# Layer 3's input transform partly as butterflies on VectorE, and y's columns moved forward

## The reference, cut to what matters

```python
x = input.reshape(-1, n)
x = fwht(x * SU_ug) / SCALE                     # n = 512
x_up   = x @ W_up.T   * (Wscale_ug[:INTER] * SCALE)
x_gate = x @ W_gate.T * (Wscale_ug[INTER:] * SCALE)
x = jax.nn.silu(x_gate) * x_up
x = fwht(x * SU_dp) / SCALE                     # n = 2048
x = x @ W_down.T * (Wscale_dp * SCALE)
```

## Time and profile before

| | us |
|---|---|
| median of 3 runs | 1746.19 |
| the runs | 1741.15 to 1750.22 |
| span of the profiled execution, first to last instruction | 1737.0 |
| TensorE busy in it | 1523.9 (88%) |
| VectorE busy | 1123.6 (65%) |
| ScalarE busy | 968.9 (56%) |
| GpSimd busy | 379.1 (22%) |

### The profile page before, as it was taken

One profiled execution on the slowest core, in us unless ns is written; L12 is line 12 of the kernel. 1 busy time (PEld: TensorE's weight loads), 2 busy tenths in 40 slices (PEclk: granted clock), 3 DMA queues, 4 the chain that ended last, 5 costly groups with the idle time before them and its releaser, 6 DMA issues.

```text
span 1737.0 us, 19550 instructions
## 1 busy us (share of the span) xinstructions
PE 1523.9 (88%) x6486; PEld 977.9 (56%) x6486; DVE 1123.6 (65%) x1830; ACT 968.9 (56%) x1270; POOL 379.1 (22%) x306
## 2 busy tenths in 40 slices
PE   5676587789995899997789999699999999999997
PEld 2222234344442456664644444378888888888886
DVE  7899488899996889995877777854322222222222
ACT  6765488889994689997347777643321221221211
POOL 0000011111110211110034545551231321321311
PEclk9898789999998899999789999889999999999999
DMA  7765633312211787763935454570110100100001
GB/s 284 267 209 187 223 115 103 110 43 79 66 39 48 210 223 182 182 164 96 367 112 182 144 184 142 196 255 13 37 37 1 37 29 9 37 15 22 1 25 73
DMA packets 102997, 206.16 MB, mean 119 GB/s; under 512 B 11060, under 2 KB 27956, under 8 KB 99188
## 3 DMA queue, kind: packets, MB, share of 16 engines
q1 hardware_dynamic: 90308, 173.72, 29.1%
q0 software_dynamic: 12592, 31.20, 8.0%
HBM read 140.13 MB, written 52.17 MB: 111 GB/s over the span
## 4 chain that ended last, share of the span: by engine, by line
PE 48%; DVE 2%; DMA 1%; ACT 1%; issue 0%; POOL 0%; SPq 0%; DVEq 0%; POOLq 0%; ACTq 0%
PE ffn_po L2502 10%; PE ffn_pg L2483 10%; PE ffn_pu L2483 10%; PE moe_psum L1890 8%; PE moe_psum L1911 4%; PE ffn_po L1584 2%; PE ffn_po L1571 2%; PE moe_psum L1829 1%; PE moe_psum L1878 1%; DVE x L2572 1%; PE moe_psum L1901 0%; DMA in_part<-expert_out,moe_source 0%; DVE x L1617 0%; DVE rt_hot_block L2183 0%; DMA rt_consts<-in_route 0%
## 5 line engine op out<-in xcount | busy, mean ns | idle before, releaser
L2405 ACT ACTIVATE up_front<-ffn_pg,ffn_gate_chunk 128x512 f32<-128x512 f32 x64 | 44.1, 689 | 320.7 <-PE ffn_pg L2483 271.7
L2562 DVE SCALAR_TENSOR_TENSOR up_front<-ffn_pu,ffn_up_scale,up_front 128x512 f32<-128x512 f32 x64 | 48.0, 751 | 231.6 <-PE ffn_pu L2483 231.5
L2572 DVE SCALAR_TENSOR_TENSOR x<-ffn_po,ffn_out_scale,x 128x512 f32<-128x512 f32 x128 | 87.2, 744 | 148.1 <-PE ffn_po L2502 148.1
L2456 POOL TENSOR_TENSOR ffn_hl<-up_front,ffn_hh 128x512 fp32r<-128x512 f32 x64 | 82.8, 1295 | 396.4 <-ACT ffn_hh L2412 396.4
L942 POOL TENSOR_TENSOR l_rr<-l_rr,constants 128x1 f32<-128x1 f32 x32 | 28.9, 903 | 487.3 <-DVE l_rr L969 487.3
L2502 PE MATMUL ffn_po<-ffn_hh,ffn_wh 128*128 128x512 f32 x256 | 101.3, 396 | 4.2 <-DVE x L2572 2.9
L2483 PE MATMUL ffn_pg<-zhi,ffn_wh 128*128 128x512 f32 x256 | 101.5, 397 | 0.5
L2483 PE MATMUL ffn_pu<-zhi,ffn_wh 128*128 128x512 f32 x256 | 100.9, 394 | 0.0
L2502 PE MATMUL ffn_po<-ffn_hh,ffn_wl 128*128 128x512 f32 x256 | 100.6, 393 | 0.0
L2483 PE MATMUL ffn_pg<-zhi,ffn_wl 128*128 128x512 f32 x256 | 100.4, 392 | 0.0
L2483 PE MATMUL ffn_pu<-zhi,ffn_wl 128*128 128x512 f32 x256 | 100.4, 392 | 0.0
(11 more groups left out here) (353 smaller groups left out, 4039.5 us busy)
## 6 DMA issues: line engine op xcount, KB each, us to landing
wkv_k<-in_fside SPq DMA_DIRECT2D x64, 256.0 KB, 4.4
ratio<-wkv_fn SPq DMA_DIRECT2D x64, 256.0 KB, 2.3
wkv_ek<-exp_k SPq DMA_DIRECT2D x48, 256.0 KB, 2.9
wkv_ekv<-exp_k_times_v SPq DMA_DIRECT2D x48, 256.0 KB, 3.5
expert_out<-moe_eo SPq DMA_DIRECT2D x39, 256.0 KB, 2.0
up_front<-in_gated SPq DMA_DIRECT2D x8, 1024.0 KB, 5.0
x<-in_x SPq DMA_DIRECT2D x4, 1024.0 KB, 7.6
down_first_a<-in_down_raw SPq DMA_DIRECT2D x16, 256.0 KB, 2.7
```

Source lines behind the costliest of these rows:

```text
L2405: eng.activation(hf[t], p_g[t][:, :], ACT.Silu, scale=scale).then_inc(*E(f"silu{t}").inc)
L2456: eng.tensor_tensor(hl[t][slot % 2][:, :], hf[t], hh[t][slot % 2][:, :].bitcast(F32), ALU.subtract).then_inc(*E(f"hl{t}").inc)
L2562: eng.scalar_tensor_tensor(hf[t], p_u[t][:, :], scale, hf[t], ALU.mult, ALU.mult).then_inc(*E(f"h{t}").inc)
L2572: last = eng.scalar_tensor_tensor(x[:, o, :], p_o[:, o, :], out_s[:, o:o + 1], x[:, o, :], ALU.mult, ALU.add)
```

## The change

The 4-point transform over the channel tiles moves from TensorE to VectorE, before the rounding. `inner` adds and subtracts tiles 0 and 1, and 2 and 3; `outer` combines the results. The sums are made in place in `g`, with the k=0 half of the diagonal matrices as spare room (these are now one allocation). ScalarE's rounding waits for `outer`, and the tiles come in the order 2, 0, 3, 1. TensorE's `fwht` keeps the 128-point part, 4 x 2 = 8 products. The matrix minus H and the instruction that made it are gone. On TensorE the columns of y of batch i+1 (`next_cols`) move from behind the "up" product of t=0 to ahead of it, for i = 0, 1 and 2.

```diff
+AS_MADE = (2, 0, 3, 1)
...
-        self.minus_H = sb("in3_minus_H", [P, P], F32R)
-        self.diag = [[sb(f"in3_diag{k}_{t}", [P, P]) for t in range(TPB)] for k in range(2)]
+        diag = sb("in3_diag", [P, 2, TPB, P])
+        self.diag = [[diag[:, k, t, :] for t in range(TPB)] for k in range(2)]
+        self.spare = diag[:, 0, :, :].rearrange("p t n -> p (t n)")
...
     def fwht(self, eng, i):
-        eng.wait_ge(*self.E("minus_H").at(0))
         eng.wait_ge(*self.E("x").at(CT * i + CT - 1))
-        for k in range(CT):
-            eng.wait_ge(*self.E("z_low").at(CT * i + k))
-            for j in range(CT):
-                h = self.minus_H if (k & j).bit_count() % 2 else self.c["H128"]
-                for t, part in enumerate((self.high(i), self.low(i))):
-                    last = eng.matmul(self.banks[:, j, :], h[:, :], part[:, k, :],
-                                      start=(k + t == 0), stop=(k == CT - 1 and t == 1))
-                if k == CT - 1:
-                    last.then_inc(*self.E("fwht").inc)
+        for n, j in enumerate(AS_MADE):
+            eng.wait_ge(*self.E("z_low").at(CT * i + n))
+            for t, part in enumerate((self.high(i), self.low(i))):
+                last = eng.matmul(self.banks[:, j, :], self.c["H128"][:, :], part[:, j, :], start=t == 0, stop=t == 1)
+            last.then_inc(*self.E("fwht").inc)
...
     def z_high(self, eng, n):
-        eng.wait_ge(*self.E("z").at(n))
-        eng.activation(self.high(n // CT)[:, n % CT, :], self.g[n % CT][:, :], ACT.Copy).then_inc(*self.E("z_high").inc)
+        k = AS_MADE[n % CT]
+        eng.wait_ge(*self.E("outer").at(n))
+        eng.activation(self.high(n // CT)[:, k, :], self.transformed(k), ACT.Copy).then_inc(*self.E("z_high").inc)
...
     def gate_and_round(self, eng, i):
         n = CT * i
-        self.gate(eng, n)
         for k in range(CT):
-            if k + 1 < CT:
-                self.gate(eng, n + k + 1)
+            self.gate(eng, n + k)
+        for k in range(CT):
             self.z_high(eng, n + k)
...
+    def inner(self, eng, i, pair):
+        eng.wait_ge(*self.E("z").at(CT * i + 2 * pair + 1))
+        if pair:
+            eng.wait_ge(*self.E("inner").at(CT * i + 1))
+        even, odd = (self.g[2 * pair + k][:, :] for k in range(2))
+        apart = self.g[1] if pair else self.spare
+        eng.tensor_tensor(apart, even, odd, ALU.subtract).then_inc(*self.E("inner").inc)
+        eng.tensor_tensor(even, even, odd, ALU.add).then_inc(*self.E("inner").inc)
+
+    def transformed(self, j):
+        return self.g[(0, 1, 3, 2)[j]][:, :]
+
+    def outer(self, eng, i):
+        eng.wait_ge(*self.E("inner").at(CT * i + CT - 1))
+        g = [t[:, :] for t in self.g]
+        eng.tensor_tensor(g[3], g[0], g[2], ALU.subtract).then_inc(*self.E("outer").inc)
+        eng.tensor_tensor(g[0], g[0], g[2], ALU.add).then_inc(*self.E("outer").inc)
+        eng.wait_ge(*self.E("outer").at(CT * i + 1))
+        eng.tensor_tensor(g[2], self.spare, g[1], ALU.subtract).then_inc(*self.E("outer").inc)
+        eng.tensor_tensor(g[1], self.spare, g[1], ALU.add).then_inc(*self.E("outer").inc)
...
     def gated(self, eng, i):
...
         self.z(eng, n + 1)
-        self.z_low(eng, n)
         self.residual(eng, n + 3)
         self.z(eng, n + 2)
-        self.z_low(eng, n + 1)
+        self.inner(eng, i, 0)
         self.z(eng, n + 3)
-        self.z_low(eng, n + 2)
-        self.z_low(eng, n + 3)
+        self.inner(eng, i, 1)
+        self.outer(eng, i)
+        for k in range(CT):
+            self.z_low(eng, n + k)
...
             product(0, 0, "gate", 0)
+            next_cols(1)
             product(0, 0, "up", 0)
-            next_cols(1)
             product(0, 0, "gate", 1)
...
             product(1, 1, "gate", 0)
+            next_cols(2)
             product(1, 1, "up", 0)
-            next_cols(2)
...
             product(2, 2, "gate", 0)
+            next_cols(3)
             product(2, 2, "up", 0)
-            next_cols(3)
```

More of the change, by code:

```diff
@@ L1523, in __init__ @@
         self.e = {}
-        self.minus_H, self.su, self.diag = start.minus_H, start.su_ug, start.diag
+        self.su, self.diag, self.spare = start.su_ug, start.diag, start.spare
         own = [start.parts, [core.sb(scope, f"in3_part{t}", [P, CH], F32)[:, :] for t in range(TPB)]]
@@ L1561, in diagonals @@
                 weight = self.c["moe_weight"][:, i * TPB + t, k:k + 1]
-                last = eng.tensor_scalar(self.diag[k][t][:, :], self.c["ident"][:, :], weight, None, ALU.mult)
+                last = eng.tensor_scalar(self.diag[k][t], self.c["ident"][:, :], weight, None, ALU.mult)
         last.then_inc(*self.E("diag").inc)
@@ L1571, in cols_of_y @@
                     last = eng.matmul(self.banks[:, o, t * P:(t + 1) * P], self.parts[i % 2][k][t][:, o * P:(o + 1) * P],
-                                      self.diag[k][t][:, :], start=k == 0, stop=k == 1)
+                                      self.diag[k][t], start=k == 0, stop=k == 1)
                 if t == TPB - 1:
@@ L1591, in gate @@
         if n >= CT:
-            eng.wait_ge(*self.E("z_low").at(n - CT))
+            eng.wait_ge(*self.E("z_low").at(n // CT * CT - 1))
         eng.activation(self.g[n % CT][:, :], self.x(n), ACT.Sigmoid).then_inc(*self.E("gate").inc)
     def z_high(self, eng, n):
-        eng.wait_ge(*self.E("z").at(n))
-        eng.activation(self.high(n // CT)[:, n % CT, :], self.g[n % CT][:, :], ACT.Copy).then_inc(*self.E("z_high").inc)
+        k = AS_MADE[n % CT]
+        eng.wait_ge(*self.E("outer").at(n))
+        eng.activation(self.high(n // CT)[:, k, :], self.transformed(k), ACT.Copy).then_inc(*self.E("z_high").inc)
     def gate_and_round(self, eng, i):
         n = CT * i
-        self.gate(eng, n)
         for k in range(CT):
-            if k + 1 < CT:
-                self.gate(eng, n + k + 1)
+            self.gate(eng, n + k)
+        for k in range(CT):
             self.z_high(eng, n + k)
     def round_transformed(self, eng, i):
-        for j in range(CT):
-            eng.wait_ge(*self.E("fwht").at(CT * i + j))
+        for n, j in enumerate(AS_MADE):
+            eng.wait_ge(*self.E("fwht").at(CT * i + n))
             eng.activation(self.high(i)[:, j, :], self.banks[:, j, :], ACT.Copy).then_inc(*self.E("high").inc)
-    def constants(self, eng):
-        eng.tensor_scalar(self.minus_H[:, :], self.c["H128"][:, :].bitcast(F32), -1.0, None, ALU.mult).then_inc(*self.E("minus_H").inc)
     def residual(self, eng, n):
@@ L1625, in z @@
         eng.scalar_tensor_tensor(g, g, self.su[:, k:k + 1], ratio, ALU.mult, ALU.mult).then_inc(*self.E("z").inc)
+    def inner(self, eng, i, pair):
[16 more added lines that the diff above has]
+        eng.tensor_tensor(g[1], self.spare, g[1], ALU.add).then_inc(*self.E("outer").inc)
     def z_low(self, eng, n):
-        k, g = n % CT, self.g[n % CT][:, :]
+        k = AS_MADE[n % CT]
         eng.wait_ge(*self.E("z_high").at(n))
-        eng.tensor_tensor(self.low(n // CT)[:, k, :], g, self.high(n // CT)[:, k, :].bitcast(F32), ALU.subtract).then_inc(*self.E("z_low").inc)
+        eng.tensor_tensor(self.low(n // CT)[:, k, :], self.transformed(k), self.high(n // CT)[:, k, :].bitcast(F32), ALU.subtract).then_inc(*self.E("z_low").inc)
     def gated(self, eng, i):
@@ L1638, in gated @@
         self.z(eng, n + 1)
-        self.z_low(eng, n)
         self.residual(eng, n + 3)
         self.z(eng, n + 2)
-        self.z_low(eng, n + 1)
+        self.inner(eng, i, 0)
         self.z(eng, n + 3)
-        self.z_low(eng, n + 2)
-        self.z_low(eng, n + 3)
+        self.inner(eng, i, 1)
+        self.outer(eng, i)
+        for k in range(CT):
+            self.z_low(eng, n + k)
     def low_transformed(self, eng, i):
-        for j in range(CT):
-            eng.wait_ge(*self.E("high").at(CT * i + j))
+        for n, j in enumerate(AS_MADE):
+            eng.wait_ge(*self.E("high").at(CT * i + n))
             eng.tensor_tensor(self.low(i)[:, j, :], self.banks[:, j, :], self.high(i)[:, j, :].bitcast(F32), ALU.subtract).then_inc(*self.E("low").inc)
@@ L2478, in product @@
                 n = 0
-                for k in range(CT):
+                for m, k in enumerate(AS_MADE):
                     if i < BATCH:
-                        eng.wait_ge(*inp.E("low").at(CT * i + k))
+                        eng.wait_ge(*inp.E("low").at(CT * i + m))
                     for part, z in ((wh, inp.zhi), (wh, inp.zlo), (wl, inp.zhi)):
```

1 line of the change is left out of this document (removed).

## The result

| | before | changed |
|---|---|---|
| median | 1743.67 us (1739.81 to 1750.22, 4 runs) | 1756.53 us (1754.65 to 1759.58, 4 runs) |
| ratio | | 1.0078, 95% interval 1.005 to 1.0105 |
| span of the profiled execution | 1737.0 | 1752.4 |

The account below looks back on a forecast made before the run. TensorE, busy 88%, bounds the kernel, but the queue order on VectorE and ScalarE decides the change: queues +8.5, clock +2.8, GpSimd +0.5, total +11.8, on span 1737.0 gives 1748.8, plus 9.2 gives 1758.0 us; range 1746 to 1765.

Parts of the forecast that it names:

- the stretch: Layer 3's input from S0 to the first product of batch 3; queues alone were forecast to lengthen it by 8.5 us.
- Rival 1: TensorE's work decides and VectorE's chain hides behind its products: 16.8 us gained, 1729.4 us; chance 0.07.
- S0 to S1: From batch 0's first product to batch 1's: forecast 32.1 us against 25.95 before, +6.1.
- S0: Start of batch 0's first product in layer 3 (S1, S2, S3: batches 1, 2, 3); forecast unshifted, near 1149.6.
- R: Start of a batch's first residual on VectorE; in batch 1 forecast at S0+13.6, where it was S0+11.58.
- S1 to S2: From batch 1's first product to batch 2's: forecast 34.7 us against 32.72 before, +2.0.
- S2 to S3: From batch 2's first product to batch 3's: forecast 33.1 us against 32.71 before, +0.4.
- The clock: TensorE's products run at 1.2 GHz in place of 2.4 after new idle stretches: +2.8 us, bounds 0 and +3.6.
- GpSimd: Its low part of batch 0's hidden tile falls among batch 1's butterflies and lengthens them: +0.5 us, bounds 0 and +1.3.
- Rival 3: GpSimd's instructions catch the butterflies in every batch: 3 x 1.3 more in place of 0.5, 1761.4 us; chance 0.11.
- The base of the sum: Span 1737.0 us plus 9.2 for launch and noise up to the median of 1746.19, to which the shift was added.
- queues: Order of VectorE's and ScalarE's instructions delays the first residuals and the transform's rounding: +8.5 us, bounds +7 and +33.

Follow-up runs that it names:

- cols_alone: Kernel before with only y's columns moved ahead of the up product of t=0, 32 products a batch, no butterflies: 1.0084 times before.
- queue: Changed kernel with VectorE's and ScalarE's queues reordered so the next batch's input stands first: 1725.96 us, 0.9951 times before.
- queue_old_transform: Kernel before with columns moved and both queues reordered, next batch's input first, but 32 products and no butterflies: 1735.10 us, 0.9996 times before.
- cols_back: Changed kernel with y's columns put back behind the up product of t=0, butterflies kept: 1.0039 times before.
- the changed kernel again: Changed kernel measured once more without any edit, on another chip: 1747.18 us, 1.0072 times before.
- keep_busy_all: Changed kernel with unread products filling TensorE's new waits, including the one behind batch 1's transform: 1745.54 us, 1.0064 times before.
- gather_later: Changed kernel with GpSimd making the low part of batch 0's hidden tile of t=0 ahead of the last gathers: 1753.43 us, single execution.
- front_only: Changed kernel with only the next batch's residuals and gates moved ahead of hidden of t=0 and its rounding: 0.9997 times before.
- back_only: Changed kernel with only the transform's rounding and low parts moved ahead of the diagonals, hidden of t=1 and its rounding: 1.005 times before.
- keep_busy: Changed kernel with unread products in TensorE's new idle stretches, but none behind batch 1's transform: 1.0082 times before.

## Why the prediction was right, point by point

The direction, the mechanism and the size held: 1758.0 was forecast and 1756.53 measured. As a shift, +11.8 was forecast, and 12.9 measured between the medians and 13.2 in the stretch. That the total is only 1.5 us off is in part luck: see the base of the sum below.

- **The product count doesn't decide.** The first residual stands directly behind `hidden` (1166.54, 1167.21), in every batch. Rival 1 asked for low parts by the end of TensorE's products; they came 9.34 us after. Its remark that residuals ahead of `hidden` would not quite do either held in queue: TensorE still waits 1.76 us ahead of batch 1's transform. cols_alone shows that the move makes the loss, queue and queue_old_transform that the count is worth 13.3 us when the queues allow it.
- **S0 to S1.** Forecast `hidden` at S0+12.92, first gate at R+2.05, product with the ratio R+2.7, low parts R+11.75, `hidden` of t=1 R+15.7, product R+18.5. Measured S0+13.28, R+2.06, R+2.8, R+13.3, R+17.3, R+20.05. The 1.5 us from the low parts on is the one butterfly beside GpSimd.
- **S1 to S2 and S2 to S3.** Forecast 34.7 and 33.1 without the clock; with the clock held 34.8 and 33.3.
- **S0.** Forecast no shift. After the first of batch 0's columns S0 came after 24.3 us before; with butterflies 24.4 in cols_back and 24.6 in the changed kernel again. The 24 products saved there (the prediction says eight, which is what is left) only became idle time. But the sign named for it, S0 near 1149.6, failed in the first profile: 1153.26, 32.0 us after the first columns. That is taken up below.
- **The clock**, forecast +2.8. 0.3 us at S0 in the first profile (`hidden` at S0+13.28) and 1.0 in the second (S0+13.9, as in keep_busy_all), each against the 12.94 of gather_later; behind S1 2.5 and 1.5. Together 2.9 and 2.5. Right in size, but part of it came at S2, not all at S1, and what S1 showed varied.
- **GpSimd**, forecast +0.5 between 0 and +1.3; measured 1.5 by the butterfly, confirmed by the run without the collision; in keep_busy_all, where a butterfly took 1.99, it is 1.3. That is at the bound or outside it. This is the term that was mis-sized. The prediction itself placed the collision among batch 1's butterflies, and then took less than half of it as if it were in doubt; by the rows it was due. That a butterfly can end over 0.5 us after GpSimd's instruction, and so lose more than its length, was not allowed for. Rival 3 (in every batch) was wrong, as argued: in batches 2 and 3 GpSimd's instruction lay in the wait for the gate. The Trainium skill's rule (SBUF — State Buffer, section "SBUF: two separate sides"), that such a pair excludes each other for the whole instruction, is supported by both traces as far as the length goes: 2.15 us beside GpSimd's instruction, 0.69 without it. The Trainium skill says there too that the one that starts first has the port for the whole instruction; the rows don't bear that out, since VectorE's starts 0.32 us before GpSimd's (1173.80, 1174.12) and is still the one that is lengthened. One collision, not three, happened.
- **The base of the sum.** I put 9.2 us between span and median. The changed kernel's profiled execution took 1754.65 us for a span of 1752.4: 2.3 us lie around the span. The other 7 were spread between executions. The base, 1746.19, was also the median of three executions; with the fourth it is 1743.67, 2.5 lower. A base 2.5 too high and a shift 1.1 too small nearly cancel in the total: what the forecast stands for is +11.8, against 12.9.

In sum 8.9 (queues) + 2.9 (clock) + 1.5 (GpSimd) make the 13.2 of the first profile but for rounding, where 8.5 + 2.8 + 0.5 were forecast. The 8.9 is what remains of keep_busy_all's 102.5, less 91.4, less 0.9 of slow products at S0 and 1.3 of GpSimd; the 2.9 is what then remains of the 13.2.

## What to carry to other kernels

Work moved earlier on one engine gains nothing unless its consumer's queue has it next: before moving it, write down what stands ahead of the consumer on its own engine, and what that waits for. Here the same move cost 12.6 us of the stretch with one order of two queues, while moved and reordered together the stretch was no longer than before (90.6 and 91.4), and 24 products a batch fewer were worth 13.3 us only there. When work goes to an engine that is far from busy, count its chain from input to output in start-to-start times, against the other engine's work in the same gap; a share of busy time doesn't say it.

## What the runs showed of the hardware

- Two profiles of the same kernel differ in the wait of batch 0. S0 came 22.2 to 24.6 us after the first columns in one group of profiles and 31.1 to 32.8 in another (the changed kernel's first, front_only, back_only, keep_busy, gather_later). The groups don't follow the edits: the changed kernel itself is in both, and the last four ran on one chip. In the changed kernel's first profile the rows show all 64 products of those columns as begun by 1131.1, and yet VectorE's first residual comes at 1136.64 and GpSimd's next gather, which waits for the same columns, at 1139.13. Both are put down to something unknown:

```profile
1136.64 0.69 DVE L1611 TENSOR_TENSOR x<-x,ffn_po 128x512 f32<-128x512 f32 x1 [16.07 <-remote]
```

  The median of the kernel before was 1743.6 to 1743.7 us in the two sets of runs that these profiles come from, and 1735.3 to 1735.7 in the other two, 8 us less. A wait for the last gather of that batch would fit; this wasn't tested and stays open.
- A wait of 3.46 us lowered the clock even behind 32 products without a pause and the eight of the transform, while in keep_busy_all, from S1 on, waits of 1.26 us and less left it at the higher level. Waits in between went both ways: the same wait of 3.41 us ahead of `down` of batch 1 is followed by some 13 products at 0.43 us from start to start in the changed kernel's first profile (1243.68) and by none in its second (1233.64).
